# Narrow cross attention: per-pair turning and normalising on the engines, or once per batch from rows that DMAs bring

## What is computed

```python
q = split_heads(query @ Wq.T + bq)
k = split_heads(key @ Wk.T + bk)
v = split_heads(value @ Wv.T + bv)
scores = jnp.einsum('bhqd,bhkd->bhqk', q, k) / np.sqrt(HEAD_DIM)
weights = jax.nn.softmax(scores, axis=-1)
out = jnp.einsum('bhqk,bhkd->bhqd', weights, v)
out = out.transpose(0, 2, 1, 3).reshape(b, -1, D_MODEL)
return out @ Wo.T + bo
```

## Time and profile before

| | us |
|---|---|
| median of 3 runs | 2075.99 (2074.86 to 2080.89) |
| the profiled execution, its own time | 2087.77 |
| its span | 2086.4 |

### The profile page before, as it was taken

The page is one execution under the profiler, slowest core; times in us unless marked ns, Lnnn a source line. Parts: engine busy times, 40 slices in busy tenths (PEclk is TensorE's granted clock), DMA queues, the critical chain, the costliest instruction groups (busy, mean ns, idle before and its releaser), DMA issues. The chain is left out here.

```text
span 2086.4 us, 33688 instructions
## 1 busy us (share of the span) xinstructions
PE 1858.2 (89%) x12989; PEld 1261.5 (60%) x12989; DVE 1518.1 (73%) x1796; ACT 1211.0 (58%) x2167; POOL 238.2 (11%) x269
## 2 busy tenths in 40 slices
PE   7988998888888884999999899999999999998764
PEld 5877785456556653778787455555555555555523
DVE  6546644379988994565653679988998998993575
ACT  1323232577677643343432178888888888884463
POOL 4313301000000001122222000010010000000000
PEclk8999998999899997999999589999999999999887
DMA  9788833157646742121213937455754755500000
GB/s 362 268 319 325 319 122 97 61 204 264 237 173 231 252 162 100 41 75 44 79 33 69 155 87 129 88 114 96 123 106 83 140 93 102 106 23 6 1 0 20
DMA packets 164206, 277.00 MB, mean 133 GB/s; under 512 B 16832, under 2 KB 92864, under 8 KB 156880
## 3 DMA queue, kind: packets, MB, share of 16 engines
q1 hardware_dynamic: 162320, 274.36, 47.0%
q10 hardware_dynamic: 1728, 0.49, 0.1%
HBM read 186.45 MB, written 88.08 MB: 132 GB/s over the span
## 5 line engine op out<-in xcount | busy, mean ns | idle before, releaser
L2142 DVE TENSOR_REDUCE xn_peaks<-psum 128x2 f32<-128x1024 f32 x512 | 623.7, 1225 | 74.6 <-PE psum L1966 69.8
L2102 ACT ACTIVATE moe_mix_transposed<-psum 128x512 f32<-128x512 f32 x1024 | 552.6, 597 | 68.5 <-PE psum L1971 31.7
L1966 PE MATMUL psum<-xn_k_words,xn_q_stack 50*128 50x512 f32 x1024 | 380.4, 464 | 5.8 <-DMA xn_q_stack<-q_rows 3.7
L1971 PE MATMUL psum<-xn_q_stack,xn_k_words 50*128 50x256 f32 x2048 | 379.3, 308 | 6.6 <-DVE xn_peaks L2142 2.9
L1971 PEld LDWEIGHTS psum<-xn_q_stack,xn_k_words 50*128 50x128 f32 x2048 | 250.9, 187 | 202.8 <-ACT moe_mix_transposed L2102 174.9
L2003 PE MATMUL psum<-moe_mix_transposed,xn_v 128*32 128x256 f32 x4096 | 329.1, 393 | 1.9 <-issue 0.3
L1966 PEld LDWEIGHTS psum<-xn_k_words,xn_q_stack 50*128 50x128 f32 x1024 | 188.1, 190 | 17.9 <-issue 14.4
L1133 DVE TENSOR_TENSOR_SCAN mx_state<-mx_decay,mx_state 128x1024 f32<-128x1024 f32 x64 | 151.4, 2366 | 4.2 <-POOL mx_decay L858 4.2
L321 PE MATMUL psum<-xw_ctx_natural,xw_weights_transposed 128*128 128x256 f32 x512 | 124.6, 389 | 12.8 <-DVE xw_weights_transposed L473 12.5
L2003 PEld LDWEIGHTS psum<-moe_mix_transposed,xn_v 128*32 128x32 f32 x4096 | 81.7, 108 | 73.8 <-issue 7.8
L723 ACT ACTIVATE ctx_k_words<-psum,ctx_bk 128x512 fp32r<-128x512 f32 x128 | 86.5, 684 | 56.8 <-PE psum L153 35.0
(11 more groups left out here) (318 smaller groups left out, 2694.3 us busy)
## 6 DMA issues: line engine op xcount, KB each, us to landing
xn_k_words<-k_words SPq DMA_DIRECT2D x384, 128.0 KB, 6.7
ctx_words<-xw_ctx_transposed_words SPq DMA_DIRECT2D x64, 512.0 KB, 7.1
ctx_chunk_words<-ctx_words SPq DMA_DIRECT2D x64, 512.0 KB, 5.3
k_words<-ctx_k_words SPq DMA_DIRECT2D x128, 256.0 KB, 2.4
v_all<-ctx_v SPq DMA_DIRECT2D x32, 544.0 KB, 3.1
xn_v<-v_all SPq DMA_DIRECT2D x32, 544.0 KB, 4.8
xw_mask<-in_mask_BxSxS_ik SPq DMA_DIRECT2D x8, 2048.0 KB, 7.6
xw_ctx_natural<-in_ctx SPq DMA_DIRECT2D x32, 512.0 KB, 6.5
```

The lines of the kernel that those rows point to most:

```text
L1966: return pe.matmul(PS[:, 2 * (x % 2) + a, :], Q[narrow_rows(a), m // XN_PAIRS % 2, m % XN_PAIRS, q * P:(q + 1) * P], K[m % XN_KSLOTS][narr ...
L1971: return pe.matmul(PS[:, narrow_bank("exp", n, step, a), half * S:(half + 1) * S], K[n % XN_KSLOTS][narrow_rows(a), kt * P:(kt + 1) * P], ...
L2102: act.activation(t["weights"][:, step % 4, a, :, :], bank.rearrange("p (t s) -> p t s", t=2), ACT.Exp, scale=XN_SCALE).then_inc(s.taken, 1)
L2142: dve.tensor_reduce(t["peaks"][:, m % 2, q, :, c], PS[:, 2 * (x % 2):2 * (x % 2) + 2, :], AX.X, ALU.max).then_inc(s.top_read, 1)
```

## The change

The results stay transposed. ACT copies the bank into one of two buffers of `sums`. SP's new `head_rows(n)`, behind the key loads of each pair, issues eight small DMAs: for each head and half, 16 rows of sums (1 KB each) go to that head's channel rows of `O`, now laid out (channel block, half, position), and one row of denominators goes to a DRAM tensor. Behind the last pair of a batch `spread_denominators(b)` waits for all of these and issues two DMAs that bring each head's denominators from DRAM to its 16 partitions. POOL adds the halves of the sums (`halves`, 128 x 512), DVE adds the halves of the denominators, takes 128 x 512 reciprocals and multiplies (`normalised`, before the maximum of step 12), and PE projects before step 15 in place of step 12. `turned`, `transposed_out`, their copies, `reciprocal_sum` and the multiplication per pair are gone. The copy of the bank waits for the DMAs of the pair before the last one.

```diff
-    if step == 3 and n:
-        uses.append(("turned", n - 1))
     if step == 4 and n % XN_PAIRS == 2 and n // XN_PAIRS + 1 < B:
         uses.append(("query", n // XN_PAIRS + 1))
     if step == 6 and n == 0:
         uses.append(("row", 0))
-    if n and n % XN_PAIRS == 0:
-        if step == 10:
-            uses.append(("out", n // XN_PAIRS - 1))
-        if step == 12:
-            uses.append(("projected", n // XN_PAIRS - 1))
+    if n and n % XN_PAIRS == 0 and step == 15:
+        uses.append(("projected", n // XN_PAIRS - 1))
...
-XN_LAST = [("turned", XN_N - 1), ("out", B - 1), ("projected", B - 1)]
+XN_LAST = [("projected", B - 1)]
...
-         "sel": sb("sum_of_halves", [P, XN_HALF]), "sums": sb("sums", [P, S]), "turned": sb("turned", [P, QT, 2, XN_W]), "rsum": sb("rsum", [P, QT, 2]),
-         }
+         "sums": sb("sums", [P, 2, S]), "denominators": sb("denominators", [P, KD, 2, S])}
...
+    def head_rows(n):
+
+        b, pair = n // XN_PAIRS, n % XN_PAIRS
+        sp.wait_ge(s.acc, n + 1)
+        if n:
+            sp.wait_ge(s.o_in, 64 * n)
+            sp.wait_ge(s.den_out, 64 * n)
+        if b and pair == 0:
+            sp.wait_ge(s.o, b)
+        for a in range(2):
+            head = 2 * pair + a
+            c, first = head * XN_DH // P, head * XN_DH % P
+            for half in range(2):
+                at = XN_W * (2 * half + a)
+                sp.dma_start(t["O"][first:first + XN_DH, c, half, :], t["sums"][at:at + XN_DH, n % 2, :]
+                             ).then_inc(s.o_in, 16)
+                sp.dma_start(Dd[b, head, half:half + 1, :], t["sums"][at + XN_DH:at + XN_VW, n % 2, :]).then_inc(s.den_out, 16)
+
+    def spread_denominators(b):
+
+        sp.wait_ge(s.den_out, 64 * XN_PAIRS * (b + 1))
+        for c in range(KD):
+            heads = Dd[b, c * P // XN_DH:(c + 1) * P // XN_DH].rearrange("h i s -> h (i s)")
+            sp.dma_start(t["denominators"][:, c, :, :].rearrange("p i s -> p (i s)"),
+                         heads[:, None, :].to_broadcast([P // XN_DH, XN_DH, 2 * S])).then_inc(s.den_in, 16)
...
+        head_rows(n)
+        if n % XN_PAIRS == XN_PAIRS - 1:
+            spread_denominators(n // XN_PAIRS)
...
-    def normalised(n):
-        b, pair = n // XN_PAIRS, n % XN_PAIRS
-        pool.wait_ge(s.rsum, n + 1)
-        if b >= 2 and pair == 0:
-            pool.wait_ge(s.made, XN_USE["out", b - 2] + 1)
-        pool.tensor_tensor(t["O"][:, b % 2, :, 2 * pair * XN_DH:2 * (pair + 1) * XN_DH].rearrange(
-            "p q (h n) -> p q h n", h=2), t["turned"][:, :, :, 0:XN_DH],
-            t["rsum"][:, :, :, None].to_broadcast([P, QT, 2, XN_DH]), ALU.mult).then_inc(s.o, 1)
+    def halves(b):
+
+        pool.wait_ge(s.o_in, 64 * XN_PAIRS * (b + 1))
+        if b:
+            pool.wait_ge(s.made, XN_USE["projected", b - 1] + 1)
+        pool.tensor_tensor(t["OT"], t["O"][:, :, 0, :], t["O"][:, :, 1, :], ALU.add).then_inc(s.halves, 1)
...
-        if n:
-            normalised(n - 1)
+        if n and n % XN_PAIRS == 0:
+            halves(n // XN_PAIRS - 1)
...
-    def turned(n):
-        free("turned", n)
-        pe.wait_ge(s.acc, n + 1)
-        for q in range(QT):
-            last = pe.matmul(PS[:, narrow_bank("turned", n), q * XN_HALF:(q + 1) * XN_HALF],
-                             t["sums"][:, q * P:(q + 1) * P], t["sel"][:], start=True, stop=True)
-        last.then_inc(s.made, 1)
-
-    def transposed_out(b):
-        free("out", b)
-        pe.wait_ge(s.o, XN_PAIRS * (b + 1))
-        for c in range(KD):
-            for q in range(QT):
-                col = (c * QT + q) * P
-                last = pe.transpose(PS[:, narrow_bank("out", b), col:col + P], t["O"][:, b % 2, q, c * P:(c + 1) * P],
-                                    k.ident[:])
-        last.then_inc(s.made, 1)
-
     def projected(b):
         free("projected", b)
-        pe.wait_ge(s.taken, XN_USE["out", b] + 1)
+        pe.wait_ge(s.o, b + 1)
...
-    def turned(n):
-        bank = made("turned", n)
-        if n:
-            act.wait_ge(s.o, n)
-        act.copy(t["turned"][:].rearrange("p q h n -> p (q h n)"), bank[:, 0:QT * XN_HALF]).then_inc(s.taken, 1)
-
-    def transposed_out(b):
-        act.copy(t["OT"].rearrange("p c s -> p (c s)"), made("out", b)).then_inc(s.taken, 1)
...
-        if n:
-            act.wait_ge(s.made, XN_USE["turned", n - 1] + 1)
-        act.copy(t["sums"][:], PS[:, XN_ACC, 0:S]).then_inc(s.acc, 1)
+        if n >= 2:
+            act.wait_ge(s.o_in, 64 * (n - 1))
+            act.wait_ge(s.den_out, 64 * (n - 1))
+        act.copy(t["sums"][:, n % 2, :], PS[:, XN_ACC, 0:S]).then_inc(s.acc, 1)
...
-    def reciprocal_sum(n):
-        dve.wait_ge(s.taken, XN_USE["turned", n] + 1)
-        if n:
-            dve.wait_ge(s.o, n)
-        dve.reciprocal(t["rsum"][:], t["turned"][:, :, :, XN_DH]).then_inc(s.rsum, 1)
+    def normalised(b):
+
+        den = t["denominators"]
+        dve.wait_ge(s.den_in, 32 * (b + 1))
+        dve.tensor_tensor(den[:, :, 0, :], den[:, :, 0, :], den[:, :, 1, :], ALU.add).then_inc(s.den, 1)
+        dve.wait_ge(s.den, 2 * b + 1)
+        dve.reciprocal(den[:, :, 0, :], den[:, :, 0, :]).then_inc(s.den, 1)
+        dve.wait_ge(s.den, 2 * b + 2)
+        dve.wait_ge(s.halves, b + 1)
+        dve.tensor_tensor(t["OT"], t["OT"], den[:, :, 0, :], ALU.mult).then_inc(s.o, 1)
...
-        if n > 0 and step == 6:
-            reciprocal_sum(n - 1)
+        if n > 0 and n % XN_PAIRS == 0 and step == 11:
+            normalised(n // XN_PAIRS - 1)
...
-    reciprocal_sum(XN_N - 2)
     ffn_weight_dve(k, 2)
-    reciprocal_sum(XN_N - 1)
+    normalised(B - 1)
```

More of the change, by code:

```diff
@@ L1702, in narrow_tiles @@
          "neg": sb("neg_max", [P, 2, QT * 2]), "neg_words": sb("neg_words", [P, QT * 2, 2], F32R),
-         "sel": sb("sum_of_halves", [P, XN_HALF]), "sums": sb("sums", [P, S]), "turned": sb("turned", [P, QT, 2, XN_W]), "rsum": sb("rsum", [P, QT, 2]),
-         }
+         "sums": sb("sums", [P, 2, S]), "denominators": sb("denominators", [P, KD, 2, S])}
     late = k.moe_mixT[:].rearrange("p e s -> p (e s)")
     t["weights"] = late[:, 0:16 * S].rearrange("p (i a t s) -> p i a t s", i=4, a=2, t=2)
-    t["O"] = late[:, 16 * S:20 * S].rearrange("p (i q d) -> p i q d", i=2, q=QT)
+    t["O"] = late[:, 16 * S:20 * S].rearrange("p (c i s) -> p c i s", c=KD, i=2)
     t["OT"] = late[:, 20 * S:22 * S].rearrange("p (c s) -> p c s", c=KD)
@@ L1714, in narrow_sems @@
 def narrow_sems(k):
-    s = k.sems("xn", "mix_pe mixed stats aggr root rstd y wq k_ones weights pads zeros made taken qlo q_out q_in top top_read neg words sum acc rsum sel o wide row plus x")
+    s = k.sems("xn", "mix_pe mixed stats aggr root rstd y wq k_ones weights pads zeros made taken qlo q_out q_in top top_read neg words sum acc o_in den_out den_in halves den o wide row plus x")
     return s, [k.xn_keys_in] + [k.sem_row(f"xn_keys{slot}_", XN_KHALVES) for slot in range(1, XN_KSLOTS)], k.sem_row("xn_values", 2)
@@ L1723, in narrow_sp @@
     vs = k.ctx_sems[0].vs
+    Dd = k.nc.dram_tensor("denominator_rows", (B, D // XN_DH, 2, S), F32, kind="Internal").ap()
     Qd = k.nc.dram_tensor("q_rows", (2, B, D, S), F32, kind="Internal").ap()
@@ L1837, in narrow_pool @@
         if n % XN_PAIRS == 1 and 0 < n // XN_PAIRS < B - 1:
-            pool.wait_ge(s.o, n - 1)
             pool.wait_ge(s.words, 2 * (n + 1))
@@ L1852, in narrow_pool @@
             pool.tensor_tensor(k.X[:, n - 1, :], k.X[:, n - 1, :], t["row"][:], ALU.add).then_inc(s.plus, 1)
-    normalised(XN_N - 1)
+    halves(B - 1)
 def narrow_pe(k, t, sems):
@@ L1944, in projected @@
         last.then_inc(s.made, 1)
-    between = {"normed": normed, "query": query, "row": row_constant, "shift": shift_rows, "turned": turned, "out": transposed_out,
-               "projected": projected}
+    between = {"normed": normed, "query": query, "row": row_constant, "shift": shift_rows, "projected": projected}
     def maxima_ready(x):
@@ L2014, in narrow_pe @@
     normed(1)
-    pe.wait_ge(s.sel, 1)
     for x in range(XN_TOP + XN_LEAD):
@@ L2186, in normed @@
                               ALU.mult).then_inc(s.y, 1)
-    dve.tensor_tensor(t["sel"][:], k.ident[:, 0:XN_HALF], k.ident[:, XN_HALF:], ALU.add).then_inc(s.sel, 1)
     mixed(0)
```

## The result

| | us |
|---|---|
| before, median of 4 runs | 2078.44 (2074.86 to 2084.34) |
| the change, median of 4 runs | 2118.49 (2110.35 to 2121.64) |
| ratio, 95% interval | 1.0170 (1.0148 to 1.0192) |
| the profiled execution of the change | 2117.81, span 2116.5 |

The change makes the kernel 1.7% slower: 31 to 40 us by the interval, 40 us between the medians. Forecast were 22 us and 2098.3 in a range of 2079 to 2118; the median lies half a microsecond above its upper end.

The account below looks back on a forecast made before the run. PE was taken to set the pace at 1.23 us per step, DVE following closely. Removed work -20.4, three batches +30.4 and the end +12.3 gave +22.3 us, 2098.3 us, in a range of 2079 to 2118.

Parts of the forecast that it names:

- DVE's arrival and the place of the wait: DVE, after the maximum of step 11, arrives 13.1 us after SP's value load and waits there for the denominators.
- Its size: DVE's wait for denominators in each batch: 3.8 us, from its arrival at 13.1 until they land at 16.9.
- The upper bound, 6.7: The second spreading DMA lands between 2.4 and 6.7 us after its issue; 2.8 was taken.
- The keys ahead of the rows: SP's queues: the small row DMAs cannot be much quicker than the key loads ahead; rows taken as landed at 13.6 us.
- The rule of order: Each DMA engine takes one ring's descriptors in order, so rows cannot overtake keys; without it rows land 0.4 us earlier.
- The rival of 0.684: DVE ahead of step 12: 512 reciprocals take as long as an addition, 0.684 us; total 2068.6 us; chance 0.08.
- the estimate of 4.3 us: DVE's 512-element reciprocal at 8.3 ns per element, 4.3 us; the sum would be 3.2 us higher.
- 0.6 are covered: Of work inserted on DVE, some 0.6 us do not stop PE; the rest does.
- The shift words: POOL's words for PE's step 14, queued behind the halves, are late, but by less than the maxima.
- The clock: PE's clock falls after each 8 us stop: 2.0 us per batch, one slow step and half the projection's extra time.
- The rival in which it stays low: PE's clock stays low for a whole pair after each stop: 15 us per batch, total 2137 us; chance 0.06.
- The end: After the fourth batch, without cover: projection starts 10.9 us later and takes 1.4 more, together 12.3 us.

Follow-up runs that it names:

- the floor: The change without row DMAs, denominators, halves and normalising, PE projecting a constant: ratio 0.9897 to the kernel before.
- the rows first: The change with SP's eight row DMAs and two spreading DMAs moved ahead of each pair's value and key loads: ratio 1.0033 to the kernel before.
- the two later runs: The change with normalising and projecting one pair later, ratio 1.0059 to the kernel before; the same also without the reciprocal, 0.9967.
- one pair later: The change with normalising and projecting moved one pair later, POOL's halves behind the shift words: ratio 1.0059 to the kernel before.
- the run without normalising: The change with its DMAs and POOL's halves but without DVE's addition, reciprocal and multiplication: ratio 0.9992 to the kernel before.

## Why the prediction was right, and where it was short

- **What bounds the kernel, and what goes.** Right: PE's steps, 1.23 us, and 20.4 us removed. The loop of the floor is 20.6 shorter.
- **DVE's arrival and the place of the wait.** Right: 13.1 us after the value load (1375.20 + 2.35 against 1364.43); with the rows first the wait went.
- **Its size.** Short: 3.8 forecast, 6.39, 6.68 and 6.86 measured. The last row DMA went out at 11.2 on that count (forecast 10.8), and the spreading ones at 14.3 (13.6). The term that was mis-sized is "the second goes out 0.5 later and lands ... after that; I take the 2.8 of the load of Wo": it went out 0.7 later and landed 4.5 us after its issue, at 19.5. The upper bound, 6.7, held. A load of the same 256 KB was a poor model for DMAs that repeat each row on 16 partitions; the DMA engines stood at a mean share of 0.47 in the middle of them (window 1382 to 1383). What made them slow was not tested.
- **The keys ahead of the rows.** Right: 3.1 us from the last row's issue to the spread behind the keys, 1.3 without them, and 6.0 against 1.8 for the rows of sums. The rule of order that the prediction cites there agrees with these rows.
- **The reciprocal.** Right: 3.46 forecast along the slope, 3.353 measured. The rival of 0.684 is refuted. So is the estimate of 4.3 us from the Trainium skill's page VectorE: DVE Perf Modes, section First, the fixed hardware budget, its repeat count read as eight cycles.
- **DVE's other work.** Short: the addition took 2.32 and 1.18 us in pairs 8 and 16, not 0.684. In both, POOL was writing zeros into the queries' stack when it began; in pair 24, where it was not, it took 0.69.
- **"0.6 are covered".** Right: ahead of step 3 it is 0.65 of 4.73 us and 0.7 of 1.4 (the two later runs). In the change, where PE's shift rows fall into the stop, about 1 us or a little more of DVE's absence is covered.
- **The shift words.** I saw that they would be late and that they hid behind the maxima; that held in the change, but I gave them no price, and they cost 8 us by the ratios, 10.6 by the loops, once DVE's part was gone.
- **The clock.** 2.0 us per batch forecast. What the two steps of a batch took beyond their ordinary 1.67 and 3.16 and beyond PE's idle time is 2.2, 2.4 and 2.0 us (pair 8: 18.81 - 4.83 - 9.81 - 1.94). Right in kind and size. The rival in which it stays low did not come. One reading was loose: in before the four matmuls end at 1209.9, and the clock is back about 2 us later.
- **The end.** 12.3 forecast, 13.0 measured. Inside it the errors are larger and of both signs: the rows landed 1.3 us after their last issue (2.4 forecast), the spread took 5.3 (3.3), and the projection 3.75 (4.16). That the total fits so well is luck.
- **Sum.** Per batch 10.1 forecast, 13.1 measured: 2.8 more of wait, 0.7 more of addition and 0.2 more of clock, less 0.6 or so that was covered. In the profiled executions loop and end cost 32 us, where 22 were forecast. The medians differ by 40; some of that is the rest of the kernel, which alone took anything from 1397.8 to 1414.3 us in the profiled executions, and one profile of each kernel cannot split it further. That the median came to lie at the upper end of the range does not confirm the way by which the prediction got there: it had put the lateness into the head rows (6.7 us after issue) and 3 us into the clock, and the runs show it in the spreading DMAs.

## What to carry to other kernels

A few small operations per unit on the bounding engine may be cheaper than one large batch operation elsewhere: the large one must fit into the slack of its engine at that place, here 0.6 to 1.0 us, and 4.7 us do not. When work leaves an engine for DMAs, count from the last input through every item ahead in the issuer's order, then give the consumer the distance in program steps; here one pair later took the wait away and cost nothing. After one wait is removed, look at the same window for the engine that was waiting behind it, and cut a long operation into pieces placed where the bounding engine is already busy.

## What the runs showed of the hardware

- RECIPROCAL on DVE has a steady price per element, not that of an addition: 0.168 us for 4, 0.453 for 48, 0.680 for 86, 1.75 for 256, 3.353 for 512 elements per partition, 6.3 ns each.
- An addition on DVE with two SBUF inputs took 2.32 us in place of 0.69, beginning at 1383.94 and ending 0.5 us after POOL's write of zeros (a cast that reads SBUF) that ran from 1383.83 to 1385.7. In pair 16 it took 1.18 and also ended 0.5 us after such a write. The Trainium skill's page SBUF — State Buffer, section SBUF: two separate sides, says that such a DVE operation and a GpSimd one that reads SBUF exclude each other, the later one waiting; the rows agree, since POOL's write had begun first, by 0.1 us in pair 8.
- 16 rows of 1 KB from SBUF to SBUF landed 6.0 us after issue behind twelve key loads and 1.8 us after issue ahead of them (medians).
- Two DMAs of 256 KB that repeat 2 KB rows from DRAM on 16 partitions each landed 4.5 us after the second's issue, with empty queues; a plain 256 KB load took 2.8.
- Inside the loop the granted clock fell to the lower level in or just behind every idle time of PE of 3.75 us and more (3.75 to 9.81). Of the two single ones of 2.15 and 2.39 us, in the run without normalising, the first lowered it and the second did not. It was back at 1.00 during the projection behind, or in the step after that.
- Two starts in one PSUM bank: with a start on the first product of each half of the positions, the second issued before the first half's sum was complete, the output was wrong; with the start on the very first product alone it was right. That the second start clears the marks of the first, so that block 1 replaces block 0, is the reading that led to the edit, and the edit bears it out; memory was not looked at.
